# Value products, row statistics and address loads moved to other places in a one-core attention and routed-experts kernel

## The chip, the cores and the metric

The kernel runs as one program on one core of a Trainium2 chip (the chip has eight). The metric is the device time of the program in microseconds, from its first instruction to its last; lower is better. Every engine of the core (TensorE or PE, VectorE or DVE, ScalarE or ACT, GpSimd or POOL) takes its own instructions in the order in which they are written, SyncE (SP) issues most DMAs, and semaphores order the engines among each other. One instruction that waits holds everything behind it on its engine.

## What is computed

Four batches of 1024 rows of 256 numbers. A first block adds gated cross attention over 77 context rows, a second one adds two of eight experts:

```python
x = x + jnp.tanh(g_xattn[0]) * _L0_xattn_ref(_layernorm(x, axis=-1), ctx_768, ...)
x = x + jnp.tanh(g_ffn[0]) * _L0_ffn_ref(_layernorm(x, axis=-1), ...)
```

`_L0_xattn_ref` normalises both inputs, forms queries, keys and values, a softmax over the 77 context rows, and projects the attended values with `Wo`. `_L0_ffn_ref` computes a softmax over eight gates, takes the two largest, and sums the two experts' outputs `relu(x @ w1[e] + b1[e]) @ w2[e] + b2[e]`, each weighted with its gate.

## The kernel before

The rows of a batch lie in 8 tiles of 128. The projections are folded into the context: `KQ` (keys times `Wq`) and `VO` (values times `Wo`, 77 x 264 for each batch), so that a tile of rows needs two transposes, a product with `KQ` (scores), a softmax, a transpose of the probabilities, and one product with `VO`. The experts' weights come as float32 and are turned into two float16 halves. The high half is written by ScalarE (`hi_part`, line 765) after a scale that comes from sums of squares (`square`, line 751, on ScalarE; `norms` on TensorE; a root, line 588, on GpSimd; `scales_start` and `scales` on VectorE, two experts at a time). The low half is written by VectorE (`lo_part`, line 1016); for two halves, named in `by_pe`, TensorE does it instead with a scaled diagonal (`lo_tools` on ScalarE, `lo_raw` and `lo_rest` on TensorE, lines 1684 and 1690) and ScalarE copies the result out (`lo_copy`, line 826).

The program has three stages. **Preparation** (to about 39 us): context, `KQ`, `VO`. **Batches one and two** (to about 138 us; they are `b` 0 and 1 in the code, and batches three and four are `b` 2 and 3): each engine walks a software pipeline, a loop over `k` in which `tile_of(b, k)` starts tile k, scores tile k-1, and so on; between these steps stand pieces of the weights' work, by hand (`if k == 4: square(2, 1)`). At the end of each batch its rows are normalised again (`mean_2`, `root_2` on GpSimd, `rows_norm_2` half on GpSimd at line 633 and half on VectorE or ScalarE), the gates are chosen (`choose_1`, `choose_2`, `gates`), places are counted (`position` on TensorE, `places` on VectorE), and the rows are split into float16 halves (`high_rows` on ScalarE, `low_rows` on VectorE, line 1273) and scattered to DRAM by expert. **Experts**: 71 slots of 128 rows, `hidden` and `output` on TensorE (lines 1815 to 1819 and 1837 to 1839) with `h_bias`, `h_hi` on ScalarE and `h_sum`, `h_low` on VectorE (lines 1468 and 1476); batches three and four go through attention in between.

What sets the order near the change is all written by hand:

- `VO`: TensorE multiplies all four batches ahead of the first tile (line 1601), VectorE adds the bias row (line 1068) and multiplies with the gate (line 1070). The products read `VT` and `Wo_s`, which lie in the place where the raw weights of experts 4 and 5 go. So SyncE holds these loads until the fourth addition:

```python
            sp.wait_ge(s_voc, B)
            sp.wait_ge(s_cc, 1)
            load_expert(4)
            load_expert(5)
            sp.wait_ge(s_lo, 1)
            load_expert(6)
            sp.wait_ge(s_lo, 2)
            load_expert(7)
            store_x1(0)
```

- VectorE computes batch two's row statistics (`stats_1(1, 0, T)`, `mean_1(1)`, lines 1031 and 1037) ahead of batch one's first tile.
- ScalarE walks from batch one's last tile through `hi_part` of expert 2, the diagonals, squares of experts 4 and 5, and `lo_copy`, to batch two's first tile (lines 849 to 858). The row copy of a tile is line 793, the exponentials are line 798, those of the gates line 830.
- After batch two TensorE runs `position(1)` and then loads addresses of weights into registers (`load_at`, `load_adr`) ahead of the first expert tile; ScalarE runs `lo_copy(1)` and `high_rows(1)` ahead of the copies of the expert rows (`rows_T`, line 914).

## Time and profile before

| | us |
|---|---|
| median of 3 runs | 595.58 (593.59 to 598.76) |
| the profiled execution | 594.17 |
| its span in the trace | 592.4 |
| PE busy | 513.9 (87%) |
| ACT busy | 425.9 (72%) |
| DVE busy | 396.0 (67%) |
| POOL busy | 276.6 (47%) |

All times below count from the start of the span. "Idle before" names how long an engine stood idle before a row and, behind the arrow, what ended it. The page's strip of the span in 40 slices (14.8 us each) shows TensorE's busy share and granted clock in tenths:

```profile
PE   6958547566989998989999989999999999999991
PEclk8985575567999999999999999999999999999997
```

The first nine slices are preparation and batches one and two; behind them TensorE is nearly always busy.

### The profile page before, as it was taken

Reading aid. Unit: us, or ns where it says so; the run is one execution under the profiler, and the core shown is the slowest. Engines: PE = TensorE matmul, PEld = TensorE weight load, DVE = VectorE, ACT = ScalarE, POOL = GpSimd, SP = SyncE. Lnnn points to the kernel's source line nnn. Section 1 sums busy time; section 2 is a strip of 40 time slices with the busy share of each in tenths; the row PEclk is TensorE's granted clock in tenths of the full one; section 3 lists DMA queues with packets and bytes.
Section 4 is the critical chain, followed back from the end, with each engine's and each line's share of the span. In section 5 each row is a group of like instructions: output and inputs, shape, how many; then the busy total and the mean of one; then the engine's idle time right before and its main releaser. Section 6 shows DMA issues by size and latency. Waiting matters only on the chain.

```text
span 592.4 us, 15755 instructions
## 1 busy us (share of the span) xinstructions
PE 513.9 (87%) x4747; PEld 426.8 (72%) x4748; DVE 396.0 (67%) x1148; ACT 425.9 (72%) x1077; POOL 276.6 (47%) x292
## 2 busy tenths in 40 slices
PE   6958547566989998989999989999999999999991
PEld 3535325335878887768888877888999998999981
DVE  3359669787876666778666777876655665665660
ACT  2649688777766675867677756887888888888870
POOL 3110334843672223968732367885775233233232
PEclk8985575567999999999999999999999999999997
DMA  6999503233633224234332232534433332332221
GB/s 170 368 381 347 195 1 98 84 120 126 180 87 63 37 29 118 30 74 103 88 60 39 65 81 38 120 93 76 85 59 52 56 47 47 56 49 46 38 28 18
DMA packets 47633, 57.07 MB, mean 96 GB/s; under 512 B 6855, under 2 KB 43197, under 8 KB 47423
## 3 DMA queue, kind: packets, MB, share of 16 engines
q1 hardware_dynamic: 32223, 36.60, 20.3%
q0 software_dynamic: 14064, 18.55, 18.1%
q10 hardware_dynamic: 1264, 0.93, 0.5%
q8 instruction: 40, 0.66, 0.5%
q14 instruction: 42, 0.34, 0.2%
HBM read 33.19 MB, written 24.49 MB: 97 GB/s over the span
## 4 chain that ended last, share of the span: by engine, by line
PE 45%; DVE 10%; issue 8%; ACT 6%; POOL 3%; DMA 2%; ACTq 1%; DVEq 1%; SPq 0%; POOLq 0%
PE hid L1815 8%; PE hid L1819 7%; PE bank L1837 6%; PE bank L1839 6%; PE bank L1838 6%; PE hid L1818 4%; PE hid L1816 4%; ACT pool L924 3%; DVE pool L1468 3%; POOL xs L599 2%; PE bank L1796 2%; PE bank L1657 2%; PE bank L1675 1%; DVE pool L1483 1%; POOL out_dram L682 1%
## 5 line engine op out<-in xcount | busy, mean ns | idle before, releaser
L682 POOL DMA_INDIRECT out_dram<-pool,idx x71 | 115.4, 1625 | 196.1 <-DVE pool L1483 156.0
L924 ACT ACTIVATE pool<-hid,b1s 128x128 f32<-128x128 f32 x568 | 168.9, 374 | 12.7 <-PE hid L1819 4.7
L1815 PE MATMUL hid<-pool,w1h 128*128 128x256 f16 x568 | 155.4, 274 | 6.5 <-DVE pool L1468 3.5
L1837 PE MATMUL bank<-w2h,pool 128*128 x568 | 154.8, 273 | 4.3 <-issue 3.7
L1819 PE MATMUL hid<-pool,w1h 128*128 128x256 f16 x568 | 155.4, 274 | 0.0
L1839 PE MATMUL bank<-w2h,pool 128*128 x568 | 154.8, 273 | 0.0
L1838 PE MATMUL bank<-w2l,pool 128*128 x568 | 154.8, 273 | 0.0
L1468 DVE TENSOR_TENSOR pool<-hid,pool 128x512 f32<-128x512 f32 x142 | 96.5, 689 | 68.6 <-ACT pool L924 68.5
L1818 PE MATMUL hid<-pool,w1l 128*128 128x128 f16 x568 | 124.8, 220 | 0.0
L1816 PE MATMUL hid<-pool,w1l 128*128 128x128 f16 x568 | 124.8, 220 | 0.0
L933 ACT ACTIVATE pool<-pool 128x512 f16<-128x512 f32 x142 | 89.9, 637 | 36.0 <-DVE pool L1468 35.6
L1476 DVE SCALAR_TENSOR_TENSOR pool<-pool 128x512 f16<-128x512 f32 x142 | 94.9, 687 | 5.2
L599 POOL DMA_INDIRECT xs<-xext,dest x64 | 72.8, 1137 | 30.7 <-issue 22.7
L1815 PEld LDWEIGHTS hid<-pool,w1h 128*128 x568 | 55.6, 98 | 15.4 <-issue 13.5
L1837 PEld LDWEIGHTS bank<-w2h,pool 128*128 128x128 f16 x568 | 55.5, 98 | 12.8 <-issue 5.4
L1818 PEld LDWEIGHTS hid<-pool,w1l 128*128 x568 | 55.7, 98 | 6.8
L1839 PEld LDWEIGHTS bank<-w2h,pool 128*128 128x128 f16 x568 | 55.5, 98 | 6.5
L1838 PEld LDWEIGHTS bank<-w2l,pool 128*128 128x128 f16 x568 | 55.5, 98 | 6.2
L1816 PEld LDWEIGHTS hid<-pool,w1l 128*128 x568 | 55.7, 98 | 4.9
L1819 PEld LDWEIGHTS hid<-pool,w1h 128*128 x568 | 55.8, 98 | 0.0
L674 POOL COPY idx<-pool 128x1 int32<-128x1 int32 x71 | 51.3, 723 | 4.0 <-DMA pool<-xs 4.0
L1483 DVE SCALAR_TENSOR_TENSOR pool<-pool,q 128x256 f32<-128x256 f32 x71 | 34.3, 484 | 26.9 <-ACT pool L940 21.3
(276 smaller groups left out, 745.7 us busy)
## 6 DMA issues: line engine op xcount, KB each, us to landing
pool<-xs SPq DMA_DIRECT2D x71, 132.5 KB, 2.3
pool<-in_L_ffn_w_dram SPq DMA_DIRECT2D x8, 1024.0 KB, 8.3
xb<-in_x_dram SPq DMA_DIRECT2D x4, 1024.0 KB, 9.5
out_dram<-xb SPq DMA_DIRECT2D x4, 1024.0 KB, 5.2
w1h<-in_L_ffn_w_dram SPq DMA_DIRECT2D x2, 1024.0 KB, 10.7
w1l<-in_L_ffn_w_dram SPq DMA_DIRECT2D x2, 1024.0 KB, 11.4
w2h<-in_L_ffn_w_dram SPq DMA_DIRECT2D x2, 1024.0 KB, 13.5
w2l<-in_L_ffn_w_dram SPq DMA_DIRECT2D x2, 1024.0 KB, 12.6
```

The source lines that it names most:

```text
L682: g.indirect_dma_start(out=out_rows, out_offset=bass.IndirectOffsetOnAxis(ap=idx[s % U][:, 0:1], axis=0), in_=y2[s % 3], in_offset=None, c ...
L924: a.activation(hb[:, c * P:(c + 1) * P], bank[c // 2][:, (2 * (c % 2) + 1) * P:2 * (c % 2 + 1) * P], ACT.Identity, bias=b1s[:, ds(e * NH + ...
L933: a.activation(hh[s % 2][:, half], hb[:, half], ACT.Relu).then_inc(g_hh, 1)
L1468: v.tensor_tensor(part, main, part, ALU.add).then_inc(g_hb, 1)
L1476: v.scalar_tensor_tensor(hl[s % 2][:, half], hb[:, half], 0.0, hh[s % 2][:, half], ALU.max, ALU.subtract).then_inc(g_hl, 1)
L1815: t.matmul(o, wh, xhl, start=True, stop=False)
L1816: t.matmul(o[:, 0:P], wl, xh, start=False, stop=False)
L1818: t.matmul(o[:, 0:P], wl, xh, start=False, stop=False)
L1819: mm = t.matmul(o, wh, xhl, start=False, stop=True)
L1837: t.matmul(o, hh[s % 2][:, hs], wh, start=c == 0, stop=False)
L1838: t.matmul(o, hh[s % 2][:, hs], wl, start=False, stop=False)
L1839: mm = t.matmul(o, hl[s % 2][:, hs], wh, start=False, stop=c == NH - 1)
```

## The change

- The products of `VO` for batches two to four leave the preparation. TensorE does them in batch one's pipeline after k = 2, 3 and 5, VectorE takes them up after k = 3, 4 and 6, in one instruction each, because the bias row is multiplied with the gate once, beforehand. They use other banks. SyncE's wait on `s_voc` is not edited.
- Batch two's row statistics move from ahead of batch one's first tile to k = 7 and 8 of its pipeline, ahead of `scales_start(1)`.
- On ScalarE the diagonals (`lo_tools(0)`) go ahead of `hi_part` of expert 2, and `hi_part` of expert 3, the gate exponentials and `lo_copy(0)` go ahead of the later squares; the scratch output of one square moves, so that `hi_part(3, 1)` needs no wait for the squares.
- On VectorE `scales_start(2)` moves into batch two's pipeline, and `low_rows(0)` goes ahead of `scales(2)`.
- Behind batch two: the half that TensorE computes is expert 6's, not expert 7's; `position(1)` goes behind the address loads; ScalarE copies the first expert rows ahead of `lo_copy(1)` and `high_rows(1)`; VectorE does `low_rows(1)` and `h_sum(0)` ahead of the last `lo_part`.

```diff
-        by_pe = (2, E - 1)
+        by_pe = (2, E - 2)
...
-        vo_bank = [0, 1, 4, 5]
+        vo_bank = [5, 6, 7, 7]
...
                 if k == 9:
+                    lo_tools(0)
                     hi_part(2, 0)
             hi_part(2, 1)
-            lo_tools(0)
             square(4, 0)
-            square(4, 1)
-            lo_copy(0)
             hi_part(3, 0)
             gate_exp(0)
+            lo_copy(0)
+            square(4, 1)
+            hi_part(3, 1)
             square(5, 0)
             square(5, 1)
-            hi_part(3, 1)
...
             gate_exp(1)
-            lo_copy(1)
-            high_rows(1, 0, T)
-
-            act.wait_ge(s_lo1, 1)
...
+            act.wait_ge(s_lo1, 1)
             rows_T(0)
+            lo_copy(1)
             rows_T(1)
-            act.wait_ge(s_lo, E - 1)
+            high_rows(1, 0, T)
             h_bias(0)
             h_hi(0)
+            act.wait_ge(s_lo, E - 1)
...
-            for b in range(B):
+            def values(b):
+                dve.wait_ge(s_vob, 1)
                 dve.wait_ge(s_vo, b + 1)
-                v.tensor_tensor(VO[0:LC, b * DX:(b + 1) * DX], bank[vo_bank[b]][0:LC, 0:DX], bor[0:LC, :], ALU.add).then_inc(s_voc, 1)
-            dve.wait_ge(s_voc, B)
-            v.tensor_scalar(VO[0:LC, :], VO[0:LC, :], tg[0:LC, 0:1], None, ALU.mult).then_inc(s_vob, 1)
+                v.scalar_tensor_tensor(VO[0:LC, b * DX:(b + 1) * DX], bank[vo_bank[b]][0:LC, 0:DX], tg[0:LC, 0:1], bor[0:LC, :],
+                                       ALU.mult, ALU.add).then_inc(s_voc, 1)
+
+            values(0)
             scales(0)
-            stats_1(1, 0, T)
-            mean_1(1)
...
+                if k in (3, 4, 6):
+                    values(k // 2)
+                if k in (7, 8):
+                    stats_1(1, (k - 7) * T // 2, (k - 6) * T // 2)
+                if k == 8:
+                    mean_1(1)
                 if k == 9:
                     scales_start(1)
...
-            scales_start(2)
             lo_part(3, 1)
 
             for k in range(T + 5):
                 tile_of(1, k)
                 if k == 1:
+                    scales_start(2)
+                    low_rows(0, 0, T)
                     scales(2)
-                    low_rows(0, 0, T)
...
-            lo_part(6, 1)
             low_rows(1, 0, T)
...
+            h_sum(0)
+            lo_part(E - 1, 1)
             dve.wait_ge(s_lo, E - 1)
-            h_sum(0)
...
             for k in range(T + 3):
                 tile_of(0, k)
+                if k in (2, 3, 5):
+                    values((k + 1) // 2)
                 if k == 8:
+                    pe.wait_ge(s_voc, B)
                     norms(1)
...
-            position(1)
...
             load_adr(0, 0)
             load_adr(0, 2 * NH)
+            position(1)
```

On TensorE, where batch one's first tiles begin (line 1601 before and 1610 after is the product of values with `Wo`, lines 1643 and 1652 turn rows, 1657 and 1666 are scores, 1664 and 1673 turn probabilities, 1675 and 1684 attend), before:

```order
L1571 MATMUL hid<-ssq,ones 128x6
L1601 MATMUL hid<-w1h,w1l 77x264 x4
L1601 MATMUL bank4<-w1h,w1l 77x264 x2
L1601 MATMUL bank5<-w1h,w1l 77x264 x2
L1643 MATMUL hid<-ident,xb0 128x128 x4
L1657 MATMUL hid<-KQ0,xT0 128x85
```

and after, from the same place on:

```order
L1575 MATMUL hid<-ssq,ones 128x6
L1610 MATMUL bank5<-w1h,w1l 77x264 x2
L1652 MATMUL hid<-ident,xb0 128x128 x4
L1666 MATMUL hid<-KQ0,xT0 128x85
L1666 MATMUL hid<-KQ1,xT0 128x85
L1652 MATMUL hid<-ident,xb0 128x128 x2
L1666 MATMUL hid<-KQ0,xT1 128x85
L1666 MATMUL hid<-KQ1,xT1 128x85
L1673 MATMUL bank4<-ident,pr0 77x128
L1610 MATMUL bank6<-w1h,w1l 77x264 x2
L1652 MATMUL hid<-ident,xb0 128x128 x2
```

Six of the eight products stand between tiles now; the first pair of them is behind the third tile's transposes.

On VectorE, at k = 7 and 8 of batch one (line 1228, after 1226, takes in the scores of a tile, 1241 and 1247, after 1239 and 1245, add the attended rows, 986, after 983, is `scales_start(1)`), before:

```order
L1228 SCALAR_TENSOR_TENSOR pr2<-hid,rs0,cst 128x77
L1229 COPY xb0<-hid 128x8
L1231 TENSOR_REDUCE nms<-pr2 128x1
L1241 RECIPROCAL rsum<-psum_p 128x1
L1247 SCALAR_TENSOR_TENSOR xb0<-bank5,rsum,xb0 128x264
L1253 BN_STATS st0<-xb0 128x6
L1228 SCALAR_TENSOR_TENSOR pr3<-hid,rs0,cst 128x77
L1229 COPY xb0<-hid 128x8
L1231 TENSOR_REDUCE nms<-pr3 128x1
```

and after:

```order
L1229 TENSOR_REDUCE nms<-pr2 128x1
L1028 BN_STATS st1<-xb1 128x6 x4
L1239 RECIPROCAL rsum<-psum_p 128x1
L1245 SCALAR_TENSOR_TENSOR xb0<-bank5,rsum,xb0 128x264
L1251 BN_STATS st0<-xb0 128x6
L1226 SCALAR_TENSOR_TENSOR pr3<-hid,rs0,cst 128x77
L1227 COPY xb0<-hid 128x8
L1229 TENSOR_REDUCE nms<-pr3 128x1
L1028 BN_STATS st1<-xb1 128x6 x4
L1032 MEMSET tick 128x1
L1034 BN_AGGR mv1<-st1 128x2 x8
L1037 TENSOR_SCALAR vv1<-mv1 128x8
```

Half of batch two's statistics stand ahead of the last tile's scores, the rest and the means ahead of `scales_start(1)`.

On ScalarE, from batch one's last tile on (765, after 763, is `hi_part`; 819 and 820, after 817 and 818, the diagonals; 751 and 755 a square; 826, after 824, `lo_copy`; 830, after 828, the gates' exponential), before:

```order
L765 ACTIVATE w1h<-w1h,scl 128x2048
L765 ACTIVATE w2h<-w1l,scl 128x2048
L819 ACTIVATE xT0<-ident,scl 128x128
L820 ACTIVATE xT1<-ident 128x128
L751 ACTIVATE w1l,ssq<-w1h 128x2048
L751 ACTIVATE w2l,ssq<-w1l 128x2048
L755 ACTIVATE bsq,ssq<-b1raw 128x8
L826 CAST w2l<-hid 128x512 x4
L765 ACTIVATE w1h<-w2h,scl 128x2048
L830 ACTIVATE ex<-lgd 128x64
```

and after:

```order
L817 ACTIVATE xT0<-ident,scl 128x128
L818 ACTIVATE xT1<-ident 128x128
L763 ACTIVATE w1h<-w1h,scl 128x2048
L763 ACTIVATE w2h<-w1l,scl 128x2048
L751 ACTIVATE w1l,ssq<-w1h 128x2048
L763 ACTIVATE w1h<-w2h,scl 128x2048
L828 ACTIVATE ex<-lgd 128x64
L824 CAST w2l<-hid 128x512 x4
L751 ACTIVATE w2l,ssq<-w1l 128x2048
```

The diagonals are ahead of the two casts of expert 2, and one cast and the exponential are ahead of the copies.

## Rows read from the trace of the kernel before

**Rows 1.** Busy time by stretch: us, PE, PEld, DVE, ACT, POOL busy, PEclk, DMA share, GB/s.
```profile
43.00:63.00 20.00, 15.48 (x52) 11.28 (x53) 17.50 (x45) 17.09 (x39) 1.64 (x1) 0.50 1.02 357
...
170.00:585.00 415.00, 396.68 (x4150) 349.07 (x4150) 275.34 (x720) 308.72 (x846) 207.88 (x209) 1.00 0.33 62
```

**Rows 2.** Chain that ended last, in order of time: start, us, what; 133 to 134 us.
```profile
133.75 1.91 ACT w2l L826 x4
```

**Rows 3.** Timeline, 34 to 44 us: start, us, engine, line, operation, idle before.
```profile
34.88 2.37 PE L1601 MATMUL bank<-w1h,w1l 128*77 128x264 f32 x8
...
37.03 1.91 ACT L751 ACTIVATE w1l<-w1h 128x2048 f16<-128x2048 f32 x1 [5.21 <-DMA w1l<-in_L_ffn_w_dram]
...
39.60 2.00 ACT L765 ACTIVATE w1h<-pool,scl 128x2048 f16<-128x2048 f32 x1 [0.30 <-DVE scl L1002]
...
39.87 2.69 DVE L1031 BATCH_NORM_STATS2 st<-xb 128x6 f32<-128x256 f32 x8
...
44.07 0.36 ACT L798 ACTIVATE pr<-pr,nms 128x77 f32<-128x77 f32 x1 [2.22 <-DVE nms L1231]
```

**Rows 4.** Groups by line, VectorE, 37 to 63 us: busy, mean ns, idle.
```profile
L1068 DVE TENSOR_TENSOR VO<-bank,w1h 77x264 f32<-77x264 f32 x1 | 0.4, 428 | 0.5 <-PE bank L1601 0.5
```

**Rows 5.** Timeline, one TensorE turn of batch one and two squares, 53 to 60 us.
```profile
53.60 1.91 ACT L751 ACTIVATE w2l<-w1l 128x2048 f16<-128x2048 f32 x1
...
57.25 1.08 PE L1675 MATMUL bank<-VO,prT 77*128 77x264 f32 x2
...
58.13 0.63 PE L1643 MATMUL hid<-ident,xb 128*128 128x128 f32 x2
...
58.76 1.15 PE L1657 MATMUL hid<-KQ,xT 128*128 128x85 f32 x4
...
59.10 1.92 ACT L751 ACTIVATE w2l<-w2l 128x2048 f16<-128x2048 f32 x1
...
59.92 1.08 PE L1675 MATMUL bank<-VO,prT 77*128 77x264 f32 x2
```

**Rows 6.** Timeline, end of batch one's tiles to the low halves, 64 to 81 us.
```profile
64.94 1.32 POOL L588 TENSOR_TENSOR nrm<-nrm,half 128x6 f32<-128x6 f32 x1 [19.77 <-DVE nrm L986]
...
67.57 2.00 ACT L765 ACTIVATE w1h<-w1h,scl 128x2048 f16<-128x2048 f32 x1 [2.59 <-DVE scl L1002]
...
68.55 0.62 SPq L480 DMA_DIRECT2D out_dram<-xb  x1
...
73.95 4.96 POOL L633 TENSOR_SCALAR xb<-xb,mv,rs 128x256 f32<-128x256 f32 x4
...
78.30 2.05 ACT L826 CAST w2l<-hid 128x512 f16<-128x512 f32 x4 [2.37 <-PE hid L1690]
```

**Rows 7.** Waits of SP's queue, 0 to 160 us: us in total, times, longest.
```profile
SPq L472 <- DVE VO L1068: 1.8, 1, 1.8
```

**Rows 8.** DMA issues, 0 to 100 us: count, KB each, us to landing.
```profile
w2l<-in_L_ffn_w_dram SPq DMA_DIRECT2D x2, 1024.0 KB, 12.6
...
out_dram<-xb SPq DMA_DIRECT2D x1, 1024.0 KB, 4.7
```

**Rows 9.** GpSimd's normalising of rows, whole span: duration ns min/median/max, first and last.
```profile
L633 POOL TENSOR_SCALAR xb<-xb,mv,rs x20: 1212/1770/2308, 73.9 to 359.2; 128x256 f32<-128x256 f32 x20
```

**Rows 10.** Timeline, batch two's first tiles, 88 to 96 us.
```profile
88.36 0.35 ACT L793 COPY xT<-hid 128x256 f32<-128x256 f32 x1
...
92.47 2.00 ACT L765 ACTIVATE w1h<-w1h,scl 128x2048 f16<-128x2048 f32 x1 [0.59 <-DVE scl L1002]
...
92.74 2.29 DVE L1273 TENSOR_TENSOR xext<-xb,xext 128x2048 f16<-128x2048 f32 x1
...
95.62 0.36 ACT L798 ACTIVATE pr<-pr,nms 128x77 f32<-128x77 f32 x1 [0.89 <-DVE nms L1231]
```

**Rows 11.** Timeline, first tiles of the experts, 135 to 146 us.
```profile
135.70 0.58 PE L1796 MATMUL bank<-ident,pool 128*128 128x128 f16 x4 [3.41 <-issue]
...
145.56 1.39 DVE L1476 SCALAR_TENSOR_TENSOR pool<-pool 128x512 f16<-128x512 f32 x2
```

More of the change, by code:

```diff
@@ L166, in gated_attention_and_routed_experts @@
         raw_turn = [1, 1, 1, 1, 1, 1, 2, 2]
-        junk = [((w1l, e), (w2l, e)) for e in range(4)] + [((w1l, 3), (w2l, 3)), ((w2h, 3), (w2l, 3)),
+        junk = [((w1l, e), (w2l, e)) for e in range(4)] + [((w1l, 3), (w2l, 3)), ((w1l, 5), (w1l, 4)),
                                                           ((w1l, 5), (w2l, 5)), ((w1l, 6), (w1l, 7))]
@@ L428, in hi_turn @@
                 return 2 * e + j + 1
-            return 2 * (E - EB) + ((1, 4), (2, 3))[e - (E - EB)][j]
+            return 2 * (E - EB) + ((1, 3), (2, 4))[e - (E - EB)][j]
         def tile_at(j):
@@ L747, in square @@
                         act.wait_ge(s_lo, e - 2)
-                elif e == 5:
-                    act.wait_ge(s_ssq, e)
+                    if e == 6:
+                        act.wait_ge(s_ssq, e)
                 w, n = junk[e][j]
@@ L759, in hi_part @@
                 act.wait_ge(s_scl, e // 2 + 1)
-                if (e, j) == (3, 1):
-                    act.wait_ge(s_ssq, 6)
                 if e >= E - 2 * EB:
@@ L882, in _ @@
             hi_part(7, 0)
+            hi_part(6, 1)
             hi_part(7, 1)
-            hi_part(6, 1)
             act.wait_ge(s_nmr, 1)
@@ L1057, in _ @@
             v.tensor_copy(bor[:, D:DX], bank[7][:, 64:64 + E]).then_inc(s_wogc, 1)
+            dve.wait_ge(s_tanh, 1)
+            dve.wait_ge(s_wogc, 2)
+            v.tensor_scalar(bor[0:LC, :], bor[0:LC, :], tg[0:LC, 0:1], None, ALU.mult).then_inc(s_vob, 1)
             dve.wait_ge(s_km, 1)
@@ L1062, in _ @@
             scales_start(0)
-            dve.wait_ge(s_tanh, 1)
-            dve.wait_ge(s_wogc, 2)
-            for b in range(B):
+            def values(b):
+                dve.wait_ge(s_vob, 1)
                 dve.wait_ge(s_vo, b + 1)
-                v.tensor_tensor(VO[0:LC, b * DX:(b + 1) * DX], bank[vo_bank[b]][0:LC, 0:DX], bor[0:LC, :], ALU.add).then_inc(s_voc, 1)
-            dve.wait_ge(s_voc, B)
-            v.tensor_scalar(VO[0:LC, :], VO[0:LC, :], tg[0:LC, 0:1], None, ALU.mult).then_inc(s_vob, 1)
+                v.scalar_tensor_tensor(VO[0:LC, b * DX:(b + 1) * DX], bank[vo_bank[b]][0:LC, 0:DX], tg[0:LC, 0:1], bor[0:LC, :],
+                                       ALU.mult, ALU.add).then_inc(s_voc, 1)
+            values(0)
             scales(0)
-            stats_1(1, 0, T)
-            mean_1(1)
             seg_n = [0]
@@ L1597, in _, with values @@
             norms(0)
-            pe.wait_ge(s_vtc, ND)
-            for b in range(B):
+            def values(b):
+                if b == 0:
+                    pe.wait_ge(s_vtc, ND)
+                if b == 1:
+                    pe.wait_ge(s_cc, 1)
+                if b == B - 1:
+                    pe.wait_ge(s_voc, b)
                 for ec in range(ND):
@@ L1603, in _ @@
                 mm.then_inc(s_vo, 1)
-            pe.wait_ge(s_cc, 1)
-            pe.wait_ge(s_voc, B)
+            values(0)
             pe.wait_ge(s_kmc, ND)
@@ L1671, in attend @@
                     else:
-                        pe.wait_ge(s_vob, 1)
+                        pe.wait_ge(s_voc, i + 1)
                 else:
```

## The prediction, made before the changed kernel ran

> **What bounds the kernel now.** I read the busy time by stretch first. From 170 to 585 us TensorE is busy 396.7 of 415 us at the full granted clock [rows 1]: the experts' stage is TensorE's own work, and the change edits nothing in it. So the change is worth what it moves the moment at which that stage starts, one for one. From 43 to 63 us, in batch one's tiles, no engine leads: VectorE is busy 17.5 of 20 us, ScalarE 17.1, TensorE 15.5 at a granted clock of 0.50, the lower of its two levels (1.2 GHz), and the DMAs run without a gap (share 1.02, 357 GB/s) [rows 1]. The chain that ended last shows in its front piece what hands over to the experts: ScalarE's copies of the low halves at 133.75 us [rows 2]. The timeline then gives each stage's place, and I lay the changed order onto it.
>
> **Start of batch one.** Before, eight products stand ahead of the tiles, the last four of them from 34.88 to 37.25 us [rows 3], then an addition and the gate on VectorE, then the first scales; ScalarE's first cast starts at 39.60 us and waits 0.30 us for those [rows 3]. But ScalarE is no earlier free: its square of expert 2 waits 5.21 us for a DMA and runs from 37.03 us [rows 3], and the first row copy stands behind it. So removing the products gains 0.3 us there. The real gain is the statistics: 2.69 us from 39.87 us on [rows 3], with the means about 3.5 us, ahead of the first tile's scores. They are why the first exponential, at 44.07 us, stood idle 2.22 us [rows 3]. Now it starts behind the second row copy, at about 41.5 us: 2.6 us early.
>
> **What batch one's pipeline gets instead.** TensorE: two products for each of three batches. The attend product has the same 264 columns and takes 0.88 us for two halves of its float32 pass (57.25 to 58.13 us [rows 5]), so two products cost 1.76 us at the lower clock, 0.88 us if the clock were the upper one. One whole turn, attend, transpose, scores, turned probabilities, is 57.25 to 59.92 us, 2.67 us [rows 5], against ScalarE's about 2.85 us for a copy, an exponential, a copy and a cast of 2.0 us [rows 3]: TensorE has 0.2 us to spare in a turn, so each insertion delays the turn behind it by up to 1.5 us, less where VectorE is later still. VectorE: three take-ups of 0.43 us [rows 4], 1.3 us, and the 3.5 us of statistics and means: 4.8 us into a stretch where it had 20 - 17.5 = 2.5 us idle [rows 1].
>
> Laid out in order, with each engine starting when its inputs and its own last instruction are done: the square of expert 2's second half comes at 52.0 us instead of 53.60 [rows 5] (1.6 early, 1.0 of the lead spent on the first two insertions), the next row copy keeps that, and the third insertion spends the rest: the second square of expert 3 comes at 59.05 us instead of 59.10 [rows 5]. At k = 7 four statistics (half of 2.69 us) delay the last tile's scores, at k = 8 the other half and the means delay everything up to `scales_start(1)`: about 67.5 us where it was just ahead of the root at 64.94 us [rows 6]. GpSimd's root of batch two's statistics now stands there too. The scales reach ScalarE at 70.7 us instead of 67.57 us [rows 6]: **3.1 us late**.
>
> **The walk to batch two.** ScalarE works from 67.57 to 88.36 us [rows 6, 10], 20.8 us, and stands idle 2.37 us in it for TensorE's low half [rows 6]. The new order closes that hole: with the diagonals first, TensorE starts at 71.3 us and is done before ScalarE gets to the copies, two casts and a square later. So 18.4 us of work, 70.7 to 89.1 us: 0.75 us late.
>
> **The loads that nobody moved.** SyncE holds the loads of experts 4 to 7 until the fourth take-up. That was no cost: 1.8 us of wait [rows 7], and the DMAs stayed full. The fourth take-up is now at k = 6, about 58.9 us. Four experts are 8.4 MB, at 357 GB/s [rows 1] 23.5 us, to 82.4 us. The squares of experts 4 and 5 (from 75 and 85 us on) still find their data. But the store of batch one's rows, issued at 68.55 us before [rows 6] and landed 4.7 us later [rows 8], now stands in the same queue behind the loads. A transfer of the same 1 MB behind others took 12.6 us [rows 8]. I take 82.4 + 2.9 = 85.3 us for its landing, 12 us later than before. GpSimd's normalising waits for it; it took 4.96 us from 73.95 us on [rows 6], now 85.3 to 90.3 us, and `high_rows(0)`, wanted at 89.4 us, waits about 1 us. Behind it VectorE now does `low_rows(0)`, 2.29 us, ahead of the scales that ScalarE's cast at 92.47 us waits for [rows 10]. That cast comes at 95.65 us, 3.2 us late. The next exponential stood idle 0.89 us [rows 10], which takes 0.9 back: **2.3 us late** through batch two, where I find no other hole that all engines share.
>
> The Trainium skill, "DMA: Bandwidth & Descriptors", section "Rules for kernel authors", says to issue a DMA early and to wait late for it. The change does the opposite here; by that rule the late loads are its cost, and the trace agrees as far as 4.7 against 12.6 us for one size goes.
>
> **The hand-over to the experts.** The address loads are the 3.41 us in which TensorE waited ahead of the first expert rows at 135.70 us [rows 11]. They now cover the wait for `position(1)`, and the rows' transpose comes about 1 us earlier, the copies of the low halves and then `hidden(0)` about 1.0 us earlier too. It is given back: `high_rows(1)` now stands ahead of `h_bias(0)`, `low_rows(1)` behind it on VectorE, and `lo_part(7, 1)`, which I take to last as long as `low_rows(0)`, 2.29 us [rows 10], between `h_sum(0)` and `h_low(0)`, which was at 145.56 us [rows 11] and comes 2.0 us later, so `output(0)` about 0.4 us. The load of the second biases also waits for that `lo_part`, and `h_sum(1)` for the load; a slot's slack hides most of it, I add 0.3 us. Sum: 2.3 + 0.4 + 0.3 = **3.0 us slower**: 594.17 + 3.0 = 597.2 us by the profiled execution, which lies 1.4 us under the median of 595.58; on the median 598.5 us.
>
> **Bounds.** If all six inserted products cost nothing (they run while TensorE waits), 1.6 us of lead stay at tile 6; if they run at the lower clock with nothing hidden, 5.3 us are added to TensorE. If the store is not behind the loads, 1.2 us go. If the slot's slack hides nothing of the late `h_sum(1)`, up to 2 us come on top.
>
> **Rivals.**
> 1. *The lead survives* (the other sign). TensorE's insertions fall into its waits and the statistics into VectorE's 2.5 us of idle time. Then the 1.6 us lead reaches the end of batch one, the hole of 2.37 us closes, and `low_rows(0)` and the hand-over cost 1.2 and 0.4 us: about 2.4 us faster, 593 us. For it: VectorE's idle time is real. Against it: the statistics come in one lump right ahead of the scales, with ScalarE already waiting 2.59 us for them [rows 6]. It decides at the cast that was at 67.57 us: if that is not late, this rival is right.
> 2. *Late loads meet GpSimd and VectorE.* Now GpSimd's four normalisings run at the same time as VectorE's two low halves of expert 3. One took 1.21 us at the least, 1.77 at the median, 2.31 at the most [rows 9], the longer ones in the experts' stage with VectorE busy beside them. Four at the most cost 4.3 us more than the four at 73.95 us [rows 6]: 3.0 + 3.5, about 6.5 us slower, 602 us. The Trainium skill, "SBUF — State Buffer", section "Who interferes with whom", says that a VectorE instruction with two inputs in SBUF contends with a GpSimd one that reads it, and that the second to come is fully blocked; by that rule this rival is right. The rows at 1.77 us bear out about half of the price.
> 3. *It cancels*: within 1 us of before, if two of the terms above (the insertions, the store) are a little smaller.
>
> **The numbers.** Forecast (1 to 6 us slower) 0.53; rival 1 0.20; rival 2 0.14; rival 3 0.10; something larger on the fast side 0.03. The range leaves out the worst of rival 2 and the fast tail: 591 to 604 us on the median; the forecast's own range is 596.5 to 601.5. About 1%, 6 us, is what a measurement of this kernel tells from no change. The forecast, rival 3 and nearly all of rival 1 lie within it: 0.79; slower by more 0.15, from rival 2 and the forecast's end; faster by more 0.06.
>
> **What would show it.** Right: the four late loads issued at 57 to 61 us with a DMA pause before; the first exponential near 41.5 us; the first cast of expert 2 near 70.7 us; no hole ahead of the low halves' copies; the store landing at 83 to 87 us; the cast of expert 4 near 95.6 us; `hidden(0)` 1 to 2 us later than before. Wrong: products that fit between the tiles without moving them, loads whose store lands at its old time, or a change in the experts' stage, which I hold for untouched.

## The result, and the profile after

Three runs of before gave 595.58 us. In the measurement that ran both kernels in turns, the changed kernel took 604.17 us (602.39 to 604.91, 4 runs) beside 596.4 us of before (593.59 to 598.76): ratio 1.0149, 95% interval 1.0104 to 1.0194. I had predicted 598.5 us in a range of 591 to 604. The sign was right, the size was not: +8 us where I had +3. Later, on other chips, the same pair was measured twice more: 1.0048 (1.0015 to 1.0081) and 1.0050 (1.0025 to 1.0076), about +3 us. That +3 us equals my forecast is luck: the traces from those chips show the same late cast as the first one (below), and not the course of the forecast. The first figure is taken apart below; why it is 8 on one chip and 3 on the others stays partly open.

The profiled execution of after took 602.39 us, with a span of 600.6 us, 8.2 us longer than before's 592.4. Its busy time by stretch (us, PE, PEld, DVE, ACT, POOL busy, PEclk, DMA share, GB/s):

```profile
43.00:63.00 20.00, 15.81 (x69) 11.80 (x69) 19.41 (x53) 16.64 (x41) 0.00 (x0) 0.76 0.23 81
63.00:85.00 22.00, 8.82 (x27) 3.45 (x25) 13.29 (x86) 17.09 (x21) 5.35 (x4) 0.66 1.02 357
85.00:100.00 15.00, 4.19 (x18) 3.35 (x18) 10.22 (x20) 4.11 (x10) 9.96 (x6) 0.50 0.00 1
170.00:585.00 415.00, 400.77 (x4195) 352.28 (x4192) 282.06 (x745) 313.12 (x859) 211.59 (x213) 1.00 0.33 63
```

The experts' stage is TensorE's as in [rows 1]. The DMAs' full stretch has moved from 43 to 63 us to 63 to 85 us. From 85 to 100 us the two engines that carry the pipeline mostly stand still, ScalarE busy 4.11 and TensorE 4.19 of 15 us, while VectorE (10.22) and GpSimd (9.96) work. That hole is the lost time, and the timeline of SP's queue shows how it comes (start, us, engine, line, operation, out<-in):

```profile
57.08 0.37 SPq L472 DMA_DIRECT2D w1h<-in_L_ffn_w_dram  x1
...
69.75 0.80 SPq L473 DMA_DIRECT2D pool<-in_L_ffn_w_dram  x1
70.60 5.07 SPq L480 DMA_DIRECT2D out_dram<-xb  x1
```

The four experts' loads are issued from 57.08 us on and the store of batch one's rows behind them. Next, the engines' timelines from 85 us on, with the idle time ahead of each row and what ended it:

```profile
85.90 8.49 POOL L633 TENSOR_SCALAR xb<-xb,mv,rs 128x256 f32<-128x256 f32 x4 [12.98 <-DMA out_dram<-xb]
...
85.82 1.62 DVE L1266 TENSOR_SCALAR xb<-xb,mv,rs 128x256 f32<-128x256 f32 x4 [7.54 <-DMA out_dram<-xb]
87.36 2.34 DVE L1013 SCALAR_TENSOR_TENSOR w1l<-w2h,scl,w1h 128x2048 f16<-128x2048 f32 x1
89.62 2.48 DVE L1013 SCALAR_TENSOR_TENSOR w2l<-w2l,scl,w2h 128x2048 f16<-128x2048 f32 x1
...
94.47 1.90 ACT L811 CAST xext<-xb 128x2048 f16<-128x2048 f32 x1 [8.04 <-issue]
...
96.47 2.29 DVE L1271 TENSOR_TENSOR xext<-xb,xext 128x2048 f16<-128x2048 f32 x1 [3.75 <-ACT xext L811]
98.68 0.15 DVE L988 SCALAR_TENSOR_TENSOR bnd<-nrm 128x2 f32<-128x2 f32 x1
...
99.84 2.00 ACT L763 ACTIVATE w1h<-w1h,scl 128x2048 f16<-128x2048 f32 x1 [2.85 <-DVE scl L999]
```

It is one chain. The store lands at about 85.8 us, 15.2 us after its issue at 70.60 us. GpSimd and VectorE both waited for it and now work side by side, and GpSimd's four normalisings take 8.49 us where they took 4.96 [rows 6]. Then ScalarE's cast of the rows, VectorE's low rows, the scales behind them, and ScalarE's cast of expert 4 at 99.84 us, which stood at 92.47 us [rows 10]. Up to the store after was even ahead: its first row copy of batch two is at 86.06 us, before's at 88.36 [rows 10].

The hand-over to the experts, VectorE and SP's queue in the timeline of after:

```profile
147.79 1.45 DVE L1471 TENSOR_TENSOR pool<-hid,pool 128x512 f32<-128x512 f32 x2
149.15 2.34 DVE L1013 SCALAR_TENSOR_TENSOR w2l<-pool,scl,w2h 128x2048 f16<-128x2048 f32 x1
...
157.72 0.16 DVE L1464 TENSOR_TENSOR q<-pool,inv 128x2 f32 x1 [2.91 <-DMA pool<-in_L_ffn_b_dram]
...
151.52 0.34 SPq L527 DMA_DIRECT2D pool<-in_L_ffn_b_dram  x1
```

The second biases' load is issued behind `lo_part(7, 1)`, at 151.52 us. The second slot's `h_sum` waits 2.91 us for it, at 157.72 us. Before, it was issued at 139.52 us and nobody waited.

### The profile page after: what moved, and what is told of

Same layout as the page of the kernel before. It is cut to its first block, busy times and chain, and to the rows that moved or that the text cites. A ratio compares the mean times of both kernels' runs of the same rounds, so it can differ in the third digit from the quotient of the medians.

```text
span 600.6 us, 15756 instructions
## 1 busy us (share of the span) xinstructions
PE 514.5 (86%) x4747; PEld 426.8 (71%) x4748; DVE 395.4 (66%) x1148; ACT 424.4 (71%) x1077; POOL 279.8 (47%) x292
## 4 chain that ended last, share of the span: by engine, by line
PE 45%; DVE 16%; issue 11%; ACT 9%; DMA 7%; SPq 6%; POOL 2%; DVEq 1%; ACTq 1%; POOLq 0%
PE hid L1826 8%; PE hid L1830 7%; PE bank L1848 6%; PE bank L1850 6%; PE bank L1849 6%; PE hid L1829 4%; PE hid L1827 4%; SPq L472 3%; ACT pool L918 3%; DVE pool L1471 3%; DMA w1l<-in_L_ffn_w_dram 2%; DVE w2l L1013 2%; PE bank L1807 2%; DMA out_dram<-pool,idx 2%; PE bank L1666 2%
```

## Experiments

Theory 1: the late store costs the time, through GpSimd beside VectorE and through the order of the low rows and scales. Theory 2: the work put between batch one's tiles costs it. The kernels of one section ran on one chip; before took 616.4, 616.0, 621.2 and 616.8 us on the four chips. Ratios to before are of 10 to 12 runs beside 23 to 35 of before, with 95% intervals; they are the measured ratios and not the quotients of the two medians. The absolute times in the first four expectations are for the first chip, where before takes 596 us; on these chips only their distances from before, or from the changed kernel, can be compared.

### First chip: one part undone at a time

Store early:

```diff
+            store_x1(0)
             sp.wait_ge(s_lo, 1)
             load_expert(6)
             sp.wait_ge(s_lo, 2)
             load_expert(7)
-            store_x1(0)
```

> The changed kernel with one line moved: SyncE issues the store of batch one's rows ahead of the loads of experts 6 and 7 instead of behind them. The value products stay between the tiles. Theory 1 (the late store did it): the store waits behind two experts' loads (4.2 MB, about 11 us at the measured 380 GB/s) less, so it lands near 74 us instead of 85.8 us, GpSimd's four normalisings take near 5 us instead of 8.49, the float16 copy of batch one's rows starts near 87 us instead of 94.47, the cast of expert 4 near 92 us instead of 99.84, and the kernel is 6 to 7 us faster than the changed one: 597 to 598 us. Theory 2 (the load of work put into batch one's tiles did it): the tiles are the same, so the time stays at 603 to 605 us.

Measured: 613.58 us, ratio 0.9962 (0.9924 to 0.9999). Value products back at the head (statistics stay between the tiles):

```diff
-                if k in (3, 4, 6):
-                    values(k // 2)
...
-                if k in (2, 3, 5):
-                    values((k + 1) // 2)
...
+            for b in range(1, B):
+                values(b)
```

> The changed kernel with all four batches' value products and take-ups back ahead of the tiles; everything else of the change stays, batch two's statistics at k = 7 and 8 too. Theory 1: the loads of experts 4 to 7 are issued near 40 us again, the store lands near 74 us, and the time is 597 to 598 us, as in the run with the store ahead. Theory 2: also faster, but by what the tiles lose (three products and take-ups, about 2 us), and no more than 602 us. If both runs come to the same time, the products between the tiles cost nothing by themselves.

Measured: 613.88 us, 0.9958 (0.992 to 0.9995). The value products alone, that is the kernel before with only these moved:

> The kernel before with the value products alone moved between the tiles; statistics, ScalarE's order, low_rows, and the hand-over to the experts are those of before. Theory 1: the fourth take-up is near 60 us, so the loads are issued there, the store lands near 86 to 88 us, GpSimd and VectorE meet, and the time is 5 to 7 us over before: 601 to 603 us. Theory 2: three products and take-ups cost 1 to 2 us: 597 to 598 us. My prediction's pricing of the late store (1.2 us) would give 597 to 599 us.

Measured: 616.07 us, 0.9998 (0.9963 to 1.0034). My theory had wanted +5 to +7 us, so this one missed. Its trace (below) has the late store and the slow normalising that I expected, and the time does not show them; this stays open. The changed kernel with the old hand-over (`by_pe` with expert 7, `lo_copy(1)` and `high_rows(1)` ahead of the rows' copies, `h_sum(0)` behind the last `lo_part`, `position(1)` ahead of the address loads):

> The changed kernel with the hand-over to the experts as before: expert 7 by TensorE, position(1) ahead of the address loads, the copies and the float16 rows ahead of the expert rows' copies, the last low half ahead of the sums. The trace of the changed kernel has hidden(0) 4.8 us late but output(0) 6.4 us late and the end 8.2 us late, with VectorE idle 2.91 us for the load of the second biases at 157.7 us. If the moved low half and the bias load behind it are a cost: 1.5 to 2.5 us faster than the changed kernel, 602 us. If the hand-over is worth nothing, as the prediction's 0.7 us nearly says: 603 to 604 us.

Measured: 620.84 us, 1.0043 (1.0006 to 1.008), beside 1.0048 and 1.0050 for the changed kernel on two later chips; the 1.5 to 2.5 us did not show. It is 7.3 us slower than the kernel with the store early on the same chip; the two differ in the store and in the hand-over.

With the store alone put early, the changed kernel is no slower than before, and with the insertions taken out too (which also makes the loads early) it is the same. GpSimd's rows of the kernel with the store early:

```profile
73.56 5.05 POOL L633 TENSOR_SCALAR xb<-xb,mv,rs 128x256 f32<-128x256 f32 x4 [2.02 <-DMA out_dram<-xb]
87.60 3.32 POOL L588 TENSOR_TENSOR nrm<-nrm,half 128x6 f32<-128x6 f32 x1 [8.98 <-DVE nrm L983]
```

The four take 5.05 us again. But the next row shows a thing I had not priced: the root ahead of the scales takes 3.32 us, 1.34 in after and 1.32 for the like one in [rows 6]. VectorE's low rows run beside it (VectorE's and ScalarE's timeline, same run):

```profile
87.43 2.28 DVE L1271 TENSOR_TENSOR xext<-xb,xext 128x2048 f16<-128x2048 f32 x1
...
92.35 2.00 ACT L763 ACTIVATE w1h<-w1h,scl 128x2048 f16<-128x2048 f32 x1 [4.42 <-DVE scl L999]
```

The low rows end at 87.43 + 2.28 = 89.71 us, the root at 87.60 + 3.32 = 90.92 us, that is 1.2 us later, nearly its own 1.34. So GpSimd seems to have stood still until VectorE was through, and the scales came late with the store early too.

### Second chip: controls, and the two halves of the price

> The kernel before, unchanged, for its profile beside the next three. The first four variants ran on a chip where it takes 616 us and not 596, and the experts' stage is the longer part there: from the first hidden product to the end 471 to 474 us in their traces, 454 in the trace of before. Expected here: the same stage beside this kernel on this chip also about 470 us, the front part as in the first trace, that is the first hidden product at 138 to 140 us. If instead its front part differed too, the stage times of the variants could not be set against the first trace. Both theories expect the same.

Its span is 614.4 us, with batch one's first exponential at 44.01 us and the cast of expert 4 at 92.01 us, as in the first trace; the experts' stage is the longer part.

> The changed kernel, unchanged, on this chip. Theory 1 (the late store costs the time by way of GpSimd, VectorE and the order of the low rows) and theory 2 (work between the tiles): ratio 1.010 to 1.019 to before, as in the first measurement. A third possibility, which the run of the values alone raised (late store, four GpSimd normalisings in 8.5 us, and yet ratio 0.9998): on this chip the front part weighs less, and the ratio is 1.005 or less. Its trace: store landed at about 85 us, cast of expert 4 at 99 us, first hidden product near 145 us minus 1.

Measured: 620.1 us, 1.0048 (1.0015 to 1.0081). Both theories missed here, and the third possibility was met: the loss at the cast of expert 4 is as large as before (table below), but the time shows less of it. VectorE's low halves in its wait for the store:

```diff
-            rows_norm_2(0, T // 2, T)
             lo_part(3, 0)
             lo_part(3, 1)
+            rows_norm_2(0, T // 2, T)
```

> Changed kernel with VectorE's two low halves of expert 3 ahead of its own half of the normalising, that is in the 7.5 us in which it waited for the store. Theory 1: the four normalisings of GpSimd then run beside four short ones of VectorE alone, as before, and take about 5 us instead of 8.5; the extended rows' cast comes at 91 us instead of 94.5, the cast of expert 4 at 96.4 instead of 99.8, and the whole is 3 to 3.5 us faster than the changed kernel (0.5 to 0.6%). Theory 2: no change, since the insertions stay; and if the 8.5 us were not due to the two low halves, GpSimd's four still take 8 us.

Measured: 616.94 us, 1.0003 (0.9974 to 1.0032), 3.2 us faster than the changed kernel beside it. Scales ahead of the low rows:

```diff
                     scales_start(2)
+                    scales(2)
                     low_rows(0, 0, T)
-                    scales(2)
```

> Changed kernel with the scales of experts 4 and 5 ahead of the low rows on VectorE, as they were before the change; everything else stays. Theory 1 with the order as its second half: the low rows wait for ScalarE's cast, which waits for the late normalising, and the scales stand behind that wait. Taken out of the wait, the scales come when GpSimd's root is done (95.7 us) plus 1.2 us: cast of expert 4 at 96.9 us instead of 99.8, the whole 2.5 to 3 us faster than the changed kernel (0.4 to 0.5%). Theory 2: no change. If the late rows themselves (store landing at 85.8 us) are the limit through the scatter of the rows and not through the scales, no change either, with the cast early and the rows' wait at the hand-over longer.

Measured: 617.55 us, 1.003 (0.9994 to 1.0066), 2.6 us faster. The first of the two in GpSimd's timeline:

```profile
85.69 5.02 POOL L633 TENSOR_SCALAR xb<-xb,mv,rs 128x256 f32<-128x256 f32 x4 [12.94 <-DMA out_dram<-xb]
90.68 1.34 POOL L588 TENSOR_TENSOR nrm<-nrm,half 128x6 f32<-128x6 f32 x1
```

The store lands as late as in after (85.69 us), GpSimd has waited as long for it (12.94 us), and the four take 5.02 us. So the 3.5 us were VectorE's two low halves beside them, not the four short normalisings of VectorE, which are still there (1.61 us).

### Third chip: the pieces together

> Changed kernel with two moves: the store of batch one's rows ahead of the loads of experts 6 and 7, and the scales of experts 4 and 5 ahead of the low rows. With the store alone moved, the trace showed the cast of expert 4 at 92.35 us waiting 4.42 us for the scales, and GpSimd's root ahead of them took 3.32 us instead of 1.34 us, beside VectorE's low rows. Theory 1: the root takes 1.3 us again, the scales come at 90.1 us, the cast 2.2 us earlier, so about 2.2 us faster than with the store alone moved: 611.4 us, ratio 0.993 to before. If the cast's wait is not what the next batch's tiles wait for: no change against the store alone (0.996).

Measured: 616.71 us, 0.9922 (0.989 to 0.9954), before at 621.2. In the trace D (table below) is 2.2 us shorter than with the store alone, as expected (5.45 against 7.66 us); the two ratios lie the same way, with intervals that overlap.

> Changed kernel with the store left late, but VectorE's two low halves of expert 3 ahead of its half of the normalising, and the scales of experts 4 and 5 ahead of the low rows. Each alone gave back 3.2 and 2.6 us. Theory 1: they are two different pieces of the price of the late store (the slow normalising; the low rows' wait ahead of the scales) and add up: cast of expert 4 at about 93.2 us, 614 to 615 us, ratio 0.996 to 0.999, as with the store early. If both remove the same wait, it stays at about 616.9 us (1.0003 to 1.003).

Measured: 617.35 us, 0.9958 (0.9926 to 0.999): with the store left late, two moves on VectorE are enough to be no slower than before. In the distances below the two pieces add up (6.5 us together, 3.4 and 3.0 alone); the times are too coarse to show it.

> The kernel with store and scales moved, and the hand-over to the experts as it was before the change. The first trace let me count 2 to 3 us for the changed hand-over, but on this chip the changed kernel (1.0048) and the one with the old hand-over (1.0043) took the same. If the hand-over costs time here: 2 to 3 us faster than the kernel with the changed one. If, as these two say, it costs nothing on this chip: within 1 us of it.

Measured: 617.1 us, 0.9937 (0.9902 to 0.9972). The median is within 1 us of the one with the new hand-over, but the intervals are wide enough to leave room for 2 us or more.

> The kernel before with only batch two's statistics moved between the tiles and the diagonals ahead of the second halves on ScalarE; value products at the head, loads and store early, scales ahead of the low rows, old hand-over. Theory 1: the insertions between the tiles cost nothing by themselves, only through the late loads; so this is as fast as the kernel before it in this call, within 1 us. Theory 2: without the six inserted products and three take-ups it is 1.5 us or more faster than that one.

Measured: 617.14 us, 0.9907 (0.9876 to 0.9938). This kernel also has the rest of ScalarE's new order, the take-up in one instruction, and `scales_start(2)` at k = 1 of batch two. The medians are equal, the ratios 0.3% apart with intervals that overlap: these runs leave up to 2 us for the insertions, and the traces narrow it (below).

### Fourth chip: the hand-over

> The kernel before, for its profile on the chip of the next two. If that chip takes about 596 us: from batch two's last exponential to the third expert slot about 51 us, as in the first trace. If it takes about 616 us: about 57 us, with TensorE waiting in the first slots for nothing that the profile shows.

Its span is 613.9 us. From batch two's last exponential to the fourth expert slot's scaled output it takes 56.1 us; 50.8 in the first trace of before, 53.7 in that of after.

> The changed kernel unchanged. If the hand-over's 2 to 3 us are hidden only where TensorE stalls by itself: on a chip where before takes 596 us ratio 1.012 to 1.017 again, on one of 616 us 1.003 to 1.008. If the first measurement simply lay high: 1.003 to 1.010 on either.

Measured: 618.99 us, 1.0050 (1.0025 to 1.0076); the same stretch 56.8 us.

> The changed kernel with the old hand-over, beside the changed one on the same chip. If the hand-over costs time: on a chip where before takes 596 us it is 2 to 3 us faster than the changed kernel; on one of 616 us within 1.5 us of it, because TensorE's own stalls in the first slots take the place of the wait. If the hand-over costs nothing: within 1.5 us on either.

Measured: 617.82 us, 1.0039 (1.0008 to 1.0069): 1.2 us below the changed kernel, inside the 1.5 us that either theory allowed here (the same stretch is 56.4 us). As this chip was one of 616 us again, neither this run nor the one before it could decide between a hand-over that costs time and one that does not.

### What the traces say together

A single profile can reach batch one up to 5 us late for a reason outside the change. From 18 to 30 us, TensorE's granted clock is 1.00 (its upper level, 2.4 GHz) in some executions and 0.50 (the lower, 1.2 GHz) in others, of one and the same program. These are the rows of that stretch in the changed kernel on the second and on the fourth chip:

```profile
18.00:30.00 12.00, 12.00 (x30) 6.83 (x29) 4.12 (x23) 5.53 (x10) 1.67 (x1) 0.50 1.09 369
```

```profile
18.00:30.00 12.00, 10.91 (x52) 7.09 (x51) 5.53 (x28) 9.37 (x15) 1.67 (x1) 1.00 1.08 371
```

Six of the seventeen profiles have the 0.50, the first of after among them, the first of before not. Four more have 0.89 to 0.92. So I read distances, not places. Column A is the first exponential of batch one; B runs from there to the first use of its scales (the insertions' stretch), C from there to batch two's first row copy (ScalarE's walk), D from there to the cast of expert 4 (store, low rows, scales); all in us.

| kernel | clock 18 to 30 us | A | B | C | D | B+C+D | GpSimd's four |
|---|---|---|---|---|---|---|---|
| before, first trace | 1.00 | 44.07 | 23.50 | 20.79 | 4.11 | 48.40 | 4.96 |
| before, 2nd chip | 0.92 | 44.01 | 23.50 | 20.39 | 4.11 | 48.00 | 4.95 |
| before, 4th chip | 0.50 | 46.26 | 23.53 | 20.22 | 4.10 | 47.85 | 4.96 |
| after, first trace | 0.50 | 41.68 | 26.30 | 18.08 | 13.78 | 58.16 | 8.49 |
| after, 2nd chip | 0.50 | 44.63 | 26.31 | 18.08 | 13.69 | 58.08 | 8.50 |
| after, 4th chip | 1.00 | 39.92 | 26.31 | 18.08 | 13.56 | 57.95 | 8.50 |
| old hand-over, first chip | 0.50 | 41.16 | 26.30 | 18.08 | 13.57 | 57.95 | 8.49 |
| old hand-over, 4th chip | 0.50 | 44.57 | 26.38 | 18.08 | 14.07 | 58.53 | 8.49 |
| store early | 1.00 | 40.30 | 26.31 | 18.08 | 7.66 | 52.05 | 5.05 |
| values at the head | 1.00 | 41.58 | 25.83 | 18.08 | 7.66 | 51.57 | 4.93 |
| values alone moved | 1.00 | 40.67 | 23.70 | 20.38 | 10.99 | 55.07 | 8.49 |
| low halves first | 0.89 | 41.48 | 26.33 | 18.08 | 10.26 | 54.67 | 5.02 |
| scales first | 1.00 | 40.05 | 26.31 | 18.08 | 10.64 | 55.03 | 8.49 |
| low halves and scales first | 0.89 | 39.97 | 26.22 | 18.08 | 7.24 | 51.54 | 5.02 |
| store early, scales first | 0.91 | 41.95 | 26.30 | 18.08 | 5.45 | 49.83 | 5.07 |
| the same, old hand-over | 0.50 | 42.97 | 26.07 | 18.09 | 5.45 | 49.61 | 5.05 |
| statistics and diagonals only | 1.00 | 41.76 | 25.83 | 18.08 | 5.45 | 49.36 | 4.93 |

The distances repeat to some tenths over chips and clocks, and every kernel's is the sum of its parts. The insertions cost 0.2 us (values alone: 23.70 against 23.50) to 0.5 us (26.31 against 25.83), the statistics 2.3 us (25.83 against 23.50), the closed hole gives 2.1 to 2.7 us in C. Of D, the low halves beside GpSimd are 3.4 us (58.08 to 54.67), the low rows ahead of the scales 3.0 us (58.08 to 55.03), and both together 6.5 us (to 51.54). From before to after on the second chip B + C + D grows by 10.1 us: 2.8 in B, 9.6 in D, less 2.3 in C. So theory 2 has fallen as the main cause. Its 2.8 us are real, but at a like clock the earlier start (column A, 44.01 to 39.92) pays for them.

The kernel with the values alone has the late store and the 8.49 us, yet its scales stand ahead of the low rows, and at the like clock its lead at A is 3.4 us. In the trace its cast of expert 4 is 3.7 us later than before's (95.74 against 92.01). Its time shows none of that. This is the result that speaks most against theory 1 as a full account of the time, and it stays open (next section).

## Why the prediction was wrong, point by point

**What bounds the kernel, and what the change can move.** Right. The experts' stage is the same, and the difference arises ahead of it.

**Start of batch one, 2.6 us early.** The place was met in after's first trace (41.68 us, I had 41.5), but by luck: TensorE's clock was at its lower level in the head there. In three profiles with this head and a clock of 1.00 the exponential comes at 39.92 to 40.30 us, 3.7 to 4.1 us early. With the statistics left at the head it is 3.4 us (40.67), with the values left there 2.3 to 2.5 (41.58, 41.76). I had given the products 0.3 us, since ScalarE waited for a DMA anyway; that DMA's wait ended at 35.60 us in the trace with 39.92, not 37.03 [rows 3].

**Batch one's pipeline, 5.7 us given back.** Too much. It gave back 2.8 us: 0.5 for the products and 2.3 for the statistics and means. I priced the products at the lower clock; from 43 to 63 us the granted clock is 0.76 in after, not 0.50 as in [rows 1]. Two products, four passes, took 1.05 us in that trace, where I had counted 1.76 us:

```profile
52.49 1.05 PE L1610 MATMUL bank<-w1h,w1l 128*77 128x264 f32 x4
```

So the scales' first use was at 67.98 us, not 70.7: 2.7 us better than my step.

**The walk to batch two, 18.4 us.** Right: 18.08 us, and the hole of 2.37 us is closed.

**The late loads.** The mechanism was right and nearly each place: issue from 57.08 us (57 to 61), landing of the store about 85.8 us (85.3). From issue to landing it took 28.7 us where I had 26.4, which used up the earlier issue. Behind that issue the landing no longer depends on the tiles, so that the scales' coming 2.7 us better than my step was worth nothing at the cast of expert 4: ScalarE was through with its walk at 86.42 us and stood idle 8.04 us.

**GpSimd's normalising, 4.96 us kept as it was. This is the step that failed.** I took the four at the price they had alone and left the price beside VectorE to rival 2, at a chance of 0.14. It came true with its own number: I had 3.5 us more, measured were 8.49 - 4.96 = 3.53. That the number fits so well is luck, for its own working, four at the longest of [rows 9], gives 4.3 us, and the 3.5 stands there without a reason. The walk from there on was right again: cast of the rows, low rows, scales, 5.45 us from the four's end to the cast of expert 4 (94.39 to 99.84), where I had 5.35 (90.3 to 95.65). So that cast came 4.2 us later than forecast, 0.5 by the store and 3.5 by GpSimd. The Trainium skill, "SBUF — State Buffer", section "Who interferes with whom", states that such a VectorE instruction contends with a GpSimd one that reads SBUF, and that who comes second of two that want the shared ports is fully blocked. As an estimate by that rule the four would be 4.7 us longer, the time from 87.36 to 92.10 us in which the two low halves run; the trace has 3.5. The root beside the low rows, 3.32 us for 1.34, agrees with it. I had let the median of [rows 9], 1.77 us, speak against the price; but the longest VectorE operation beside any of those 20 normalisings takes 0.71 us, so those rows could not show the price of one of 2.3 us. The trace of before did show it elsewhere, and I had not looked there: GpSimd's root of batch one's second statistics (line 625) starts 0.17 us behind a low half and takes 3.67 us; the one of batch two starts 0.01 us ahead of a low half and takes 1.67 us.

```profile
69.97 2.34 DVE L1016 SCALAR_TENSOR_TENSOR w1l<-w1h,scl 128x2048 f16<-128x2048 f32 x1
70.14 3.67 POOL L625 TENSOR_TENSOR rs<-vv,neghalf 128x8 f32<-128x8 f32 x1 [3.89 <-DVE vv L1261]
...
125.98 1.67 POOL L625 TENSOR_TENSOR rs<-vv,neghalf 128x8 f32<-128x8 f32 x1 [0.73 <-DVE vv L1261]
125.99 2.35 DVE L1016 SCALAR_TENSOR_TENSOR w1l<-pool,scl,w1h 128x2048 f16<-128x2048 f32 x1
```

Two microseconds for one low half: that row of before, times two, would have priced the four within half a microsecond.

**Low rows ahead of the scales.** I counted it as part of the walk, but not as avoidable: 3.0 us of D hang on it, by its wait for the late cast and, with the store early, by the blocked root.

**Through batch two, 0.9 us taken back.** 1.2 us: 7.4 us late at the cast, 6.1 at the diagonals (123.47 to 129.60 us).

**The hand-over, 0.7 us.** In the first pair of traces 2.1 us, 6.1 to 8.2. The first half held and gave more than the 1 us forecast: the rows' transpose, 140.18 us, is 4.5 us later than before's 135.70 [rows 11], so 1.6 us regained. The biases' load was the mis-sized term: I gave it 0.3 us, `h_sum(1)` waited 2.91 us.

**Sum.** 3.0 us forecast, 8.2 us in the trace: 4.2 at the cast of expert 4, less 0.3 in batch two, plus 1.4 at the hand-over (rounded). Rival 2 with its 602 us was the best of my cases, and short by little more than the hand-over. Of the forecast error, the 3.5 us on GpSimd are shown by two experiments that end the meeting in different ways (low halves first: 5.02 us, and 3.2 us off the time; store early: 5.05 us). The hand-over's share rests on one pair of traces alone. And in that pair the two heads ran at different clocks. At 1.00 the same head gave its exponential at 39.92 us on the fourth chip, 1.8 us before the 41.68 us here, so up to that much of the 8.2 us may be no cost of the change.

**What stays open.** On the later chips the change costs 3 us and not 8, and of two pairs that differ in the hand-over alone the old one is 0.4 us slower (third chip) and 1.2 us faster (fourth), both inside the scatter. At a like clock (0.92 and 1.00) the cast of expert 4 is 5.9 us late there too (92.01 to 97.87; before on the second chip, after on the fourth), and the span of that execution is only 2.9 us longer (614.4 to 617.3). On these chips the experts' stage loses time by itself: from 170 to 300 us TensorE is busy 123.0 us in the first trace of before and 114.9 us in the second chip's. There, TensorE in the first slot's output (start, us, idle before):

```profile
148.63 0.27 PE L1839 MATMUL bank<-w2h,pool 128*128 x1
148.73 0.27 PE L1837 MATMUL bank<-w2h,pool 128*128 x1
149.38 0.27 PE L1838 MATMUL bank<-w2l,pool 128*128 x1 [0.37 <-issue]
150.11 0.27 PE L1839 MATMUL bank<-w2h,pool 128*128 x1 [0.46 <-issue]
150.81 0.27 PE L1837 MATMUL bank<-w2h,pool 128*128 x1 [0.44 <-issue]
```

Products that elsewhere follow each other in 0.11 us come 0.7 us apart, at an engine that waits for nothing the profile shows. Before's first scaled output (line 940) comes 13.4 us after the first bias on its hidden rows (line 924) there, 9.7 us in the first trace; after's 14.3 us in both. So it may be that where TensorE stalls the old hand-over is as slow as the new one, and the 2 to 3 us vanish. The traces fit that, but no run shows it by taking the stalls away. At batch two's diagonals the same two executions are 4.6 us apart (123.03 and 127.64), at the end 2.9; but from there to the end the profiles of before and after on the second and fourth chip scatter between 488.8 and 491.4 us, so those 1.7 us have no place.

Two more numbers don't close. The values alone are 3.7 us late at the cast of expert 4 and 0.0 us (-2.3 to +2.1) in the time. And the statistics and diagonals only are 0.9 us early there (91.12 against 92.01) and 0.9% (0.6 to 1.2%) faster in the time, some 4 us more than the trace shows. The head's clock, which a single profile shows in one of its two states and the median mixes, may hold part of both; this was not tried.

## What to carry to other kernels

When a transfer moves behind others, price everything that waits for its landing as it will then run, with its new neighbours on the shared memory ports, and not as it ran alone. A lead that is won between the issue of a transfer and its landing is worth nothing to what waits for the landing: look for such a moment first. And before a price is set aside for want of rows, look for the same pair of neighbours anywhere in the trace: here the root at 70.14 us. Two lines (the store ahead of two loads, the scales ahead of the low rows) turn a kernel that was 0.5 to 1.5% slower than before on three chips into one that was 0.8% faster on another (0.9922, 0.989 to 0.9954). The kernel with only the statistics and ScalarE's new order, without moved products, is as fast (0.9907), so most of that gain doesn't come from the products.

## What I had not expected of the hardware

- GpSimd's work is stretched beside VectorE operations with two large operands: four normalisings went from 4.96 to 8.49 us beside two of them, a root of 1.34 us to 3.32 us beside one of 2.28 us. Who starts first matters for the root of line 625: 3.67 us when VectorE was 0.17 us ahead (all three traces of before), 1.64 to 1.67 us when it was itself 0.01 to 0.02 us ahead of VectorE's low half (three such places in the first two traces). The normalisings don't show it so cleanly: the second of the four in after starts 0.07 us ahead of the low half and still takes 3.34 us.
- TensorE's granted clock in the first 40 us differs between executions of the same program (0.50 or 1.00 from 18 to 30 us). With it goes a later first exponential of batch one, but not by one amount: with the changed kernel's head it came at 39.92 to 40.30 us at 1.00, 39.97 to 41.95 us at 0.89 to 0.91, and 41.16 to 44.63 us at 0.50; before's at 44.01 and 44.07 against 46.26 us. Two single profiles are comparable only after this is looked up.
- One kernel took 596 us on one chip and 616 to 621 us on others, by 17 us or more in the experts' stage, where TensorE's product stream stops for 0.4 us at a time.
